# One expert's weights multiplied from split FP32R halves instead of FP32, in a fused attention and mixture-of-experts kernel

## The chip, the cores and the metric

The kernel runs on one core of a Trainium2 chip. The metric is the device time of one execution in microseconds. TensorE does the matrix products, VectorE, ScalarE and GpSimd do elementwise work, and SyncE (SP) issues most DMAs. Each engine works through its own instruction queue in order; between engines there are only semaphores.

## The reference

The input x has 4 x 1024 tokens of 256 features. It is normalised (layer norm), then three terms are added:

```python
xn = _layernorm(x, axis=-1)
x = x + _L0_attn_ref(xn, Wq, Wk, Wv) + _L0_ffn_ref(xn, w_gate, w_in, w_out)
```

The attention has 16 heads of 16 features, softmax over the keys, and a normalisation over each batch entry. The feed-forward part has 8 experts without a nonlinearity between their two layers, and each token takes the two experts with the highest logits:

```python
for e in range(E):
    h = xt @ w_in[e].T                       # hidden 1024
    y = y + gates[:, e:e + 1] * (h @ w_out[e].T)
```

Because nothing stands between the two products, the kernel multiplies the two weight matrices of an expert first (256 x 1024 by 1024 x 256) and applies the 256 x 256 composite to the tokens.

## The kernel before

**Tiling.** The tokens are 32 tiles of 128, in 8 chunks of 4 tiles. An expert's hidden dimension of 1024 is cut into two halves of 512; half i = 2e + s is one w_in tile and one w_out tile of 128 partitions x 1024 elements in FP32 (512 KB each). They land in one of 6 slots, made of the tiles wp and of the parts of xn and acc that belong to chunks 4 to 7, which are not needed yet.

**The stage of the experts.** expert_product(e, s) (L952) multiplies one half: for each of the two 128-row blocks of the composite (dh) it runs HU = 4 FP32 matmuls of 256 columns (L960), accumulating over both halves in one bank of PSUM. half_done counts finished first halves, m_ready counts finished blocks of the composite. ScalarE (m_out, L486) copies a block out rounded to FP32R, and VectorE (m_lo, L671) subtracts to get the low part, so that later products can be done as three FP32R matmuls: high x high, high x low, low x high.

**What lies between the products.** The first two chunks of tokens are handled in the same stage: token_statistics and normalise_tokens on VectorE with scale_of_chunk on GpSimd (L394) between, transposes on TensorE (L921), xt_out on ScalarE and xt_lo on VectorE, which split the transposed tokens into xth and xtl, and project_v (L948) and project_qk (L932), which are FP32R in three terms, with copies by v_out and qk_copy on ScalarE and qk_lo_half on VectorE. TensorE's order in this stage is written out by hand (L968 to L993): products 0 and 1, transposes of chunk 0, product 2, project_v of chunk 0, two blocks of project_qk, product 3, two more blocks, product 4, transposes of chunk 1, product 5, project_v of chunk 1, product 6, two blocks, product 7, two blocks, then products 8 to 15 with nothing between. ScalarE, VectorE and GpSimd have orders of their own that fit this (L538 to L559, L773 to L804, L400).

**Loads.** SP's load_weights (L278) issues the two DMAs of half i and, from i = 6 on, first waits until the product of half i - 6 is done.

**After the stage.** TensorE waits for ml_done of all experts and goes on with y_bank (L1007), the tokens times the composites, mixed with the projections of chunks 2 to 7; then attention (L1039, L1061, L1081) over 32 blocks. The tiles qf and kf hold the attention's features; GpSimd sets kf to 1.0 at the start (L392), and SP's first feature loads come after all experts.

**Tiles.** qf (128 x 4 x 1024, FP32R), kf (128 x 4 x 512, FP32R) and the third set of xth and xtl (chunk 2) are not in use while the experts' weights are multiplied.

Of the kernel before, what the change touches and what calls it, by code (L numbers as in the profile page):

```python
# [15 lines left out]
def attention_and_experts(nc, x, wq_t, wk_t, wv_t, wg_t, w_in, w_out_t, out):  # L16
# [29 lines left out]
    HELD = 4  # L46
    SETS = 3
# [10 lines left out]
    with ctx:  # L58
# [57 lines left out]
        WS = len(win)  # L116
        vb = sb("vb", [P, 2, NKT, VW])
# [55 lines left out]
        half_done = sem("half_done")  # L173
        m_ready = sem("m_ready")
# [98 lines left out]
        def _(sp):  # L273
# [108 lines left out]
        def _(pool):  # L382
# [9 lines left out]
            nc.gpsimd.memset(kf[:].bitcast(FP32), 1.0).then_inc(att_const, 1)  # L392

# [6 lines left out]
            for c in range(NC // 2):  # L400
                scale_of_chunk(c)
# [74 lines left out]
        def _(act):  # L476
# [4 lines left out]

            def m_out(e):
# [6 lines left out]
            def xt_out(c):  # L489

                if c >= SETS:
                    act.wait_ge(y_ready[-1], TC * (c - SETS + 1))
                for kt in range(KT):
# [43 lines left out]

            xt_out(0)  # L538
            m_out(0)
            for t in range(TC):  # L540
                v_out(0, t)
            for o in range(2):
                qk_copy(0, o)
            m_out(1)
            for o in range(2, 4):
                qk_copy(0, o)
            xt_out(1)
            m_out(2)
            for t in range(TC):
                v_out(1, t)  # L550
            for o in range(2):
                qk_copy(1, o)
            m_out(3)
            for o in range(2, 4):
                qk_copy(1, o)
            m_out(4)
            second_weight(0)
            for e in range(5, E):
                m_out(e)  # L559

# [65 lines left out]
        def _(dve):  # L626
# [31 lines left out]
            def xt_lo(c):  # L658
# [118 lines left out]
            nc.vector.tensor_tensor(wqkl[:], wqk, wqkh[:].bitcast(FP32), ALU.subtract).then_inc(w_lo, 1)  # L777
            xt_lo(0)
            m_lo(0)
            token_statistics(1)  # L780
            normalise_tokens(1)
            for o in range(2):
                qk_lo_half(0, o)
            m_lo(1)
            for o in range(2, 4):
                qk_lo_half(0, o)
            xt_lo(1)
            m_lo(2)
            token_statistics(2)
            normalise_tokens(2)  # L790
            for o in range(2):
                qk_lo_half(1, o)
            m_lo(3)
            for o in range(2, 4):
                qk_lo_half(1, o)
            dve.wait_ge(const_step, 6 + E)
            first_choice(0)
            second_choice(0)
            m_lo(4)
            gate_weights(0)  # L800
            token_statistics(3)
            normalise_tokens(3)
            for e in range(5, E):
                m_lo(e)  # L804
# [109 lines left out]
        def _(pe):  # L914
# [37 lines left out]
            def expert_product(e, s):  # L952

                slot = (2 * e + s) % WS
                pe.wait_ge(w_in_s[slot], 32 * ((2 * e + s) // WS + 1))
                for dh in range(KT):
                    if s == 0 and e >= 2:
                        pe.wait_ge(ml_done, KT * (e - 2) + dh + 1)
                    for h in range(HU):
                        last = nc.tensor.matmul(ps[:, M_BANK[e % 2][dh], 0:D], win[slot][:, h, dh * P:(dh + 1) * P],  # L960
                                                wout[slot][:, h, :], start=s == 0 and h == 0,
                                                stop=s == 1 and h == HU - 1)
# [226 lines left out]
```

## Time and profile before

| | us |
|---|---|
| median of 3 runs (1003.32 to 1004.2) | 1004.07 |
| profiled execution | 1001.28 |
| its span, first to last instruction | 999.5 |
| TensorE busy in the span | 974.0 |
| VectorE, ScalarE, GpSimd busy | 780.2, 694.2, 285.1 |

The profiled execution is a single one and 2.8 us below the median of the runs. All durations in the rows further down are from it. A row of a timeline has the start, the length, the engine, the line of the kernel, the operation and, in brackets, how long the engine had been idle and what released it. PE is TensorE, PEld its load of weights, DVE VectorE, ACT ScalarE, POOL GpSimd, SPq and ACTq the issue of DMAs. An FP32 matmul appears as two records.

### The profile page before, as it was taken

To read this page: it belongs to the slowest core of one execution; us is meant where nothing else is said; L and a number is where in the kernel's file an instruction comes from. 1 tells how busy PE (TensorE), PEld (TensorE's weight loads), DVE (VectorE), ACT (ScalarE), POOL (GpSimd) and SP (SyncE) were. 2 spreads that over 40 slices of the span, in tenths; PEclk is the share of its full clock that TensorE was granted. 3 is DMA by queue.
4 is the path that set the end of the run, shared out by engine and by line. 5 is a ranking of instruction groups with operands and counts; after the bars stand their busy time and mean duration, and the time that the engine had idled before them with its cause. 6 is when DMAs were issued, how large, how long until landed. Compare 5 with 4: busy or idle time off the path is not lost.

```text
span 999.5 us, 20786 instructions
## 1 busy us (share of the span) xinstructions
PE 974.0 (97%) x7816; PEld 504.5 (50%) x7816; DVE 780.2 (78%) x961; ACT 694.2 (69%) x1385; POOL 285.1 (29%) x389
## 2 busy tenths in 40 slices
PE   7999999999998999999999999999999999999994
PEld 6888888888876433333333333333333333333332
DVE  4344454543466899999999999999999999999975
ACT  2312333333322789999989899898989999899994
POOL 2001445544455222223222322223222322223222
PEclk9999999999999999999999999999999999999997
DMA  9967442223200133333333333333333333332204
GB/s 355 366 248 217 144 139 76 72 78 107 88 23 1 43 98 92 97 92 95 92 93 95 88 100 87 97 92 93 94 91 99 86 98 92 95 93 73 73 23 162
DMA packets 127043, 108.59 MB, mean 109 GB/s; under 512 B 81120, under 2 KB 102368, under 8 KB 126944
## 3 DMA queue, kind: packets, MB, share of 16 engines
q1 hardware_dynamic: 122720, 102.81, 35.4%
q10 hardware_dynamic: 4224, 4.46, 1.3%
q8 instruction: 62, 1.02, 0.4%
q14 instruction: 37, 0.30, 0.1%
HBM read 80.75 MB, written 42.21 MB: 123 GB/s over the span
## 4 chain that ended last, share of the span: by engine, by line
PE 96%; POOL 1%; DMA 1%; DVE 1%; issue 1%; ACT 0%; DVEq 0%; SPq 0%; ACTq 0%; POOLq 0%
PE ps L1081 28%; PE ps L1061 22%; PE ps L1007 18%; PE ps L1039 11%; PE ps L960 6%; PE ps L932 4%; PE ps L948 2%; PE ps L1097 1%; PE ps L1109 1%; PE ps L921 1%; DMA wp<-w_out_t 0%; DMA qf<-ot 0%; POOL rden L425 0%; ACT stage L534 0%; DVE xn L885 0%
## 5 line engine op out<-in xcount | busy, mean ns | idle before, releaser
L750 DVE TENSOR_REDUCE negm<-ps 128x1 f32<-128x1024 f32 x512 | 614.8, 1222 | 31.7 <-PE ps L1039 27.3
L585 ACT ACTIVATE wp<-ps 128x512 f32<-128x512 f32 x680 | 368.9, 595 | 43.7 <-PE ps L1061 6.7
L1061 PE MATMUL ps<-qf,kf 50*128 50x512 f32 x1024 | 373.1, 446 | 0.1
L1039 PE MATMUL ps<-kf,qf 48*128 48x512 f32 x1024 | 366.1, 444 | 1.0 <-DVE negm L750 1.0
L1061 PEld LDWEIGHTS ps<-qf,kf 50*128 50x128 f32 x1024 | 152.6, 185 | 199.0 <-ACT wp L585 97.5
L1081 PE MATMUL ps<-wp,vb 128*17 128x256 f32 x2720 | 212.6, 385 | 0.1
L1039 PEld LDWEIGHTS ps<-kf,qf 48*128 48x128 f32 x1024 | 147.2, 185 | 4.3 <-issue 3.9
L425 POOL TENSOR_TENSOR rden<-choice,minus 128x16 f32<-128x16 f32 x31 | 90.3, 2914 | 151.5 <-ACT choice L604 151.5
L585 ACT ACTIVATE picks<-ps 128x512 f32<-128x512 f32 x172 | 102.7, 597 | 22.8 <-PE ps L1061 5.0
L741 DVE SCALAR_TENSOR_TENSOR acc<-ps,gates,acc 128x256 f32<-128x256 f32 x64 | 30.8, 482 | 101.3 <-PE ps L1007 97.2
L1081 PEld LDWEIGHTS ps<-wp,vb 128*17 128x17 f32 x2720 | 46.0, 95 | 122.7 <-ACT vstage L585 53.2
L440 POOL TENSOR_TENSOR mpart<-negm,zero 128x8 fp32r<-128x8 f32 x64 | 12.9, 201 | 321.3 <-DVE negm L750 321.3
L1007 PE MATMUL ps<-mth,xth 128*128 128x512 f32 x256 | 102.6, 401 | 1.2 <-DVE stage L739 0.5
L585 ACT ACTIVATE vstage<-ps 128x512 f32<-128x512 f32 x172 | 101.8, 592 | 1.1 <-PE ps L1061 1.1
L1007 PE MATMUL ps<-mth,xtl 128*128 128x512 f32 x256 | 101.0, 395 | 0.0
L1007 PE MATMUL ps<-mtl,xth 128*128 128x512 f32 x256 | 100.9, 394 | 0.0
L534 ACT ACTIVATE wp<-ps,gates 128x256 f32<-128x256 f32 x96 | 40.3, 471 | 51.1 <-PE ps L1007 51.1
L521 ACT CAST stage<-ps 128x512 fp32r<-128x512 f32 x32 | 18.8, 587 | 60.2 <-PE ps L932 51.2
L1007 PEld LDWEIGHTS ps<-mth,xth 128*128 128x128 f32 x256 | 48.1, 188 | 14.4 <-issue 4.8
L1081 PE MATMUL ps<-picks,vb 128*17 128x256 f32 x688 | 53.9, 385 | 0.9 <-issue 0.8
L408 POOL TENSOR_TENSOR wp<-wp 128x512 f32<-128x512 f32 x24 | 31.1, 1294 | 82.8 <-ACT wp L534 82.8
L1007 PEld LDWEIGHTS ps<-mth,xtl 128*128 128x128 f32 x256 | 48.1, 188 | 11.5
(124 smaller groups left out, 898.9 us busy)
## 6 DMA issues: line engine op xcount, KB each, us to landing
qk_d<-stage SPq DMA_DIRECT2D x64, 256.0 KB
feat_d<-qk_d SPq DMA_DIRECT2D x64, 256.0 KB, 3.3
qf<-feat_d SPq DMA_DIRECT2D x128, 128.0 KB
qf<-feat_d SPq DMA_DIRECT2D x128, 64.0 KB
kf<-feat_d SPq DMA_DIRECT2D x128, 64.0 KB
v_d<-vstage ACTq DMA_DIRECT2D x8, 544.0 KB, 4.8
vb<-v_d SPq DMA_DIRECT2D x128, 34.0 KB, 2.4
acc<-x SPq DMA_DIRECT2D x8, 512.0 KB, 7.2
```

The source lines that it names most:

```text
L408: nc.gpsimd.tensor_tensor(scaled[:, 0:2], scaled[:, 0:2], scaled[:, 2:4], ALU.add).then_inc(ff_step, 1)
L425: nc.gpsimd.tensor_tensor(rden[:], rows[:, :, :, DH], minus[:], ALU.pow).then_inc(rows_step, 1)
L534: nc.scalar.activation(sums_of(t)[0][:, 2 * (j - BY_VECTOR) + h, :], ps[:, y_bank_of(t, j), h * D:(h + 1) * D], ACT.Copy, scale=gates[:, t ...
L585: nc.scalar.activation(weight_tile(n, j, b)[:, h * HALF:(h + 1) * HALF], ps[:, score_bank(score_turn[unit, b]), :], ACT.Exp).then_inc(exp_ ...
L741: nc.vector.scalar_tensor_tensor(out=total, in0=product, scalar=gate, in1=total, op0=ALU.mult, op1=ALU.add).then_inc(ff_added[j], 1)
L750: nc.vector.tensor_reduce(negm[:, n % 2, qt:qt + 1], ps[:, b:b + 2, :].rearrange("p b c -> p (b c)"), AX.X, ALU.max, negate=True).then_inc ...
L932: last = nc.tensor.matmul(ps[:, PROJECT_BANK[o % 2], :], w[:, o // 2, kt, (o % 2) * P:(o % 2 + 1) * P], v[:, c % SETS, kt, :], start=i == ...
L960: last = nc.tensor.matmul(ps[:, M_BANK[e % 2][dh], 0:D], win[slot][:, h, dh * P:(dh + 1) * P], wout[slot][:, h, :], start=s == 0 and h == ...
L1007: last = nc.tensor.matmul(ps[:, y_bank_of(t, j), :], v[:, t // TC % SETS, kt, tokens], m[:, kt, 2 * j:2 * j + 2, :].rearrange("p e d -> p ...
L1039: last = nc.tensor.matmul(ps[:, MAX_BANK[turn % 2] + half, :], qf[rows, u, qt * P:(qt + 1) * P], kf[rows, u, :], start=True, stop=True)
L1061: nc.tensor.matmul(ps[:, score_bank(score_turn[unit, half]), :], kf[rows, u, j * P:(j + 1) * P], qf[rows, u, h * HALF:(h + 1) * HALF], sta ...
L1081: last = nc.tensor.matmul(ps[32 * c:32 * c + VW, PV_BANK, 0:POS // 4], vb[:, n % 2, j + b * NKT // 2, :], weight_tile(n, j, b)[:, c * (POS ...
```

## The change

Only half 0 of the first expert stays in FP32 (WHOLE = 1). The other fifteen halves are split into a high part, rounded to FP32R, and a low part, and multiplied in three FP32R terms (24 matmuls of 256 columns in place of 8 FP32 ones). There are two sets of split tiles, used in turn: the four slots of qf, and kf with the third set of xth and xtl. ScalarE makes the high parts, GpSimd the low part of w_in, VectorE the low part of w_out. The loads wait for the split of half i - 6 instead of its product. The orders of ScalarE, VectorE and GpSimd are written anew, and GpSimd's memset of kf moves behind the last product. The order of TensorE stays.

```diff
+        flat_kf = kf[:].rearrange("p s k -> p (s k)")
+        split = [[qf[:, i, :] for i in range(4)],
+                 [flat_kf[:, 0:POS], flat_kf[:, POS:2 * POS], xth[:, SETS - 1].rearrange("p k t -> p (k t)"),
+                  xtl[:, SETS - 1].rearrange("p k t -> p (k t)")]]
...
-                if earlier >= 0:
-                    sp.wait_ge(*((m_ready, KT * (earlier // 2 + 1)) if earlier % 2 else (half_done, earlier // 2 + 1)))
+                if 0 <= earlier < WHOLE:
+                    sp.wait_ge(*((m_ready, KT) if earlier else (half_done, 1)))
+                elif earlier > 0:
+                    sp.wait_ge(w_in_low, earlier - WHOLE + 1)
+                    sp.wait_ge(w_out_low, earlier - WHOLE + 1)
...
-            nc.gpsimd.memset(kf[:].bitcast(FP32), 1.0).then_inc(att_const, 1)
...
-            for c in range(NC // 2):
-                scale_of_chunk(c)
+            def low_of_w_in(i):
+                pool.wait_ge(w_high, 2 * (i - WHOLE) + 1)
+                high, low = split[i % 2][0:2]
+                nc.gpsimd.tensor_tensor(low, win[i % WS], high.bitcast(FP32), ALU.subtract).then_inc(w_in_low, 1)
+
+            scaled_after = {0: 0, 2: 1, 6: 2, 9: 3}
+            for i in range(2 * E):
+                if i >= WHOLE:
+                    low_of_w_in(i)
+                if i in scaled_after:
+                    scale_of_chunk(scaled_after[i])
+            pool.wait_ge(m_ready, KT * E)
+            nc.gpsimd.memset(kf[:].bitcast(FP32), 1.0).then_inc(att_const, 1)
...
+            def high_of_weights(i):
+                slot = i % WS
+                act.wait_ge(w_in_s[slot], 32 * (i // WS + 1))
+                if i >= WHOLE + 2:
+                    act.wait_ge(*((m_ready, KT * ((i - 2) // 2 + 1)) if i % 2 else (half_done, (i - 2) // 2 + 1)))
+                nc.scalar.copy(split[i % 2][0], win[slot]).then_inc(w_high, 1)
+                nc.scalar.copy(split[i % 2][2], wout[slot]).then_inc(w_high, 1)
...
+            def low_of_w_out(i):
+                dve.wait_ge(w_high, 2 * (i - WHOLE) + 2)
+                high, low = split[i % 2][2:4]
+                nc.vector.tensor_tensor(low, wout[i % WS], high.bitcast(FP32), ALU.subtract).then_inc(w_out_low, 1)
...
             def expert_product(e, s):
+                i = 2 * e + s
+                if i < WHOLE:
+                    pe.wait_ge(w_in_s[i], 32)
+                    products = [(win[i], wout[i], h) for h in range(HU)]
+                else:
+                    pe.wait_ge(w_in_low, i - WHOLE + 1)
+                    pe.wait_ge(w_out_low, i - WHOLE + 1)
+                    in_high, in_low, out_high, out_low = split[i % 2]
+                    products = [(a, b, h) for h in range(HU) for a, b in ((in_high, out_high), (in_high, out_low), (in_low, out_high))]
```

ScalarE's order becomes, with high(i) for high_of_weights(i): high(1), xt_out(0), high(2), m_out(0), v_out(0, 0..3), high(3), qk_copy(0, 0..1), high(4), m_out(1), qk_copy(0, 2..3), high(5), xt_out(1), high(6), m_out(2), v_out(1, 0..3), high(7), qk_copy(1, 0..1), high(8), m_out(3), qk_copy(1, 2..3), high(9), high(10), m_out(4), then for e = 5, 6, 7: high(2e + 1), high(2e + 2) if there is one, m_out(e), with second_weight(0) after m_out(6).

VectorE's order becomes, with low(i) for low_of_w_out(i): low(1), xt_lo(0), low(2), m_lo(0), statistics and normalisation of chunk 1, low(3), qk_lo_half(0, 0..1), low(4), m_lo(1), qk_lo_half(0, 2..3), low(5), xt_lo(1), low(6), m_lo(2), statistics and normalisation of chunk 2, low(7), qk_lo_half(1, 0..1), low(8), m_lo(3), qk_lo_half(1, 2..3), low(9), token_statistics(3), low(10), m_lo(4), normalise_tokens(3), low(11), first_choice(0), low(12), m_lo(5), second_choice(0), low(13), low(14), m_lo(6), low(15), gate_weights(0), m_lo(7).

## Rows read from the trace of the kernel before

**Rows 1.** The page: busy time of each engine; the last chain by engine.

```profile
PE 974.0 (97%) x7816; PEld 504.5 (50%) x7816; DVE 780.2 (78%) x961; ACT 694.2 (69%) x1385; POOL 285.1 (29%) x389
...
PE 96%; POOL 1%; DMA 1%; DVE 1%; issue 1%; ACT 0%; DVEq 0%; SPq 0%; ACTq 0%; POOLq 0%
```

**Rows 2.** The chain that ended last, in order of time: start, length, what.

```profile
16.10 0.87 PE ps L921 x8
...
20.43 3.07 PE ps L948 x24
...
46.91 2.79 PE ps L932 x12
49.69 3.45 PE ps L960 x16
...
84.48 1.09 PE ps L921 x8
...
95.43 0.73 PE ps L948 x6
```

**Rows 3.** Table by stretches: busy us of PE, PEld, DVE, ACT, POOL; clock; DMA.

```profile
25.00:50.00 25.00, 25.00 (x129) 21.82 (x128) 9.35 (x25) 7.54 (x20) 1.21 (x2) 1.00 0.96 366
50.00:75.00 25.00, 25.00 (x117) 21.80 (x116) 12.08 (x42) 3.87 (x11) 1.21 (x2) 1.00 0.69 248
```

**Rows 4.** Groups of ScalarE by shape, 0 to 220 us: busy us, mean ns.

```profile
L495 ACT CAST xth<-ps 128x512 fp32r<-128x512 f32 x14 | 7.5, 594 | 9.8 <-PE ps L921 9.8
...
L486 ACT CAST mth<-ps 128x256 fp32r<-128x256 f32 x16 | 5.9, 376 | 31.8 <-PE ps L960 31.8
...
L480 ACT CAST wqkh<-stage 128x1024 fp32r<-128x1024 f32 x1 | 1.0, 1040 | 0.0
```

**Rows 5.** The timeline of VectorE: start, length, what, idle time before.

```profile
13.20 1.22 DVE L777 TENSOR_TENSOR wqkl<-stage,wqkh 128x1024 fp32r<-128x1024 f32 x1
...
65.03 1.41 DVE L633 BATCH_NORM_STATS2 st<-acc 128x6 f32<-128x256 f32 x4
...
67.09 0.16 DVE L645 SCALAR_TENSOR_TENSOR var<-part 128x4 f32<-128x4 f32 x1
```

**Rows 6.** GpSimd's additions by line: ns min/median/max.

```profile
L408 POOL TENSOR_TENSOR wp<-wp x24: 1287/1296/1299, 93.3 to 276.0; 128x512 f32<-128x512 f32 x24
...
L416 POOL TENSOR_TENSOR acc<-acc,wp x24: 729/738/847, 96.4 to 279.1; 128x256 f32<-128x256 f32 x24
```

**Rows 7.** The timeline at the kernel's end, VectorE and GpSimd, 993 to 997 us.

```profile
993.71 0.69 DVE L911 TENSOR_TENSOR stage<-xn,acc 128x512 f32<-128x512 f32 x1
...
994.08 1.44 POOL L472 TENSOR_TENSOR stage<-xn,acc 128x512 f32<-128x512 f32 x1 [1.19 <-ACT xn L622]
...
994.67 1.40 DVE L911 TENSOR_TENSOR stage<-xn,acc 128x512 f32<-128x512 f32 x1 [0.28 <-ACT xn L622]
```

**Rows 8.** The timeline of TensorE's weight loads in products 0 and 1.

```profile
6.08 6.05 PEld L960 LDWEIGHTS ps<-wp 128*128 128x128 f32 x16 [6.08 <-DMA wp<-w_out_t]
12.38 3.32 PEld L960 LDWEIGHTS ps<-wp 128*128 128x128 f32 x16 [0.24 <-DMA wp<-w_out_t]
```

**Rows 9.** The timeline of GpSimd after the stage of the experts.

```profile
92.07 0.20 POOL L396 TENSOR_TENSOR veps<-var,epst 128x4 f32<-128x4 f32 x1 [23.46 <-DVE var L645]
92.35 1.01 POOL L398 TENSOR_TENSOR rstd<-veps,mhalf 128x4 f32<-128x4 f32 x1
```

**Rows 10.** Table by stretches: product 0 (L960's PE and PEld), then the kernel's end.

```profile
7.00:8.00 1.00, 1.00 (x4) 0.73 (x4) 1.00 1.00 310
...
985.00:986.00 1.00, 0.39 (x4) 0.15 (x2) 1.00 (x2) 0.00 (x0) 0.00 (x0) 1.00 0.00 0
986.00:987.00 1.00, 0.00 (x0) 0.00 (x0) 0.97 (x2) 0.00 (x0) 0.00 (x0) 1.00 0.39 140
...
988.00:989.00 1.00, 0.00 (x0) 0.00 (x0) 0.28 (x1) 0.00 (x0) 0.64 (x1) 0.50 0.44 155
```

**Rows 11.** The timeline of SP's DMA issues: the first load of features.

```profile
94.58 1.51 SPq L325 DMA_DIRECT2D qf<-feat_d  x2
```

More of the change, by code:

```diff
@@ L46, in attention_and_experts @@
     HELD = 4
+    WHOLE = 1
     SETS = 3
@@ L116, in attention_and_experts @@
         WS = len(win)
+        flat_kf = kf[:].rearrange("p s k -> p (s k)")
+        split = [[qf[:, i, :] for i in range(4)],
+                 [flat_kf[:, 0:POS], flat_kf[:, POS:2 * POS], xth[:, SETS - 1].rearrange("p k t -> p (k t)"),
+                  xtl[:, SETS - 1].rearrange("p k t -> p (k t)")]]
+        split = [[part.rearrange("p (h d) -> p h d", h=HU) for part in parts] for parts in split]
         vb = sb("vb", [P, 2, NKT, VW])
@@ L173, in attention_and_experts @@
         half_done = sem("half_done")
+        w_high = sem("w_high")
+        w_in_low = sem("w_in_low")
+        w_out_low = sem("w_out_low")
         m_ready = sem("m_ready")
@@ L546, in _ @@
                 qk_copy(0, o)
+            high_of_weights(5)
             xt_out(1)
+            high_of_weights(6)
             m_out(2)
@@ L555, in _ @@
                 qk_copy(1, o)
+            high_of_weights(9)
+            high_of_weights(10)
             m_out(4)
-            second_weight(0)
             for e in range(5, E):
+                high_of_weights(2 * e + 1)
+                if e + 1 < E:
+                    high_of_weights(2 * e + 2)
                 m_out(e)
+                if e == E - 2:
+                    second_weight(0)
             for t in range(NT - 1):
@@ L777, in _ @@
             nc.vector.tensor_tensor(wqkl[:], wqk, wqkh[:].bitcast(FP32), ALU.subtract).then_inc(w_lo, 1)
+            low_of_w_out(1)
             xt_lo(0)
+            low_of_w_out(2)
             m_lo(0)
@@ L781, in _ @@
             normalise_tokens(1)
+            low_of_w_out(3)
             for o in range(2):
                 qk_lo_half(0, o)
+            low_of_w_out(4)
             m_lo(1)
@@ L786, in _ @@
                 qk_lo_half(0, o)
+            low_of_w_out(5)
             xt_lo(1)
+            low_of_w_out(6)
             m_lo(2)
@@ L790, in _ @@
             normalise_tokens(2)
+            low_of_w_out(7)
             for o in range(2):
                 qk_lo_half(1, o)
+            low_of_w_out(8)
             m_lo(3)
@@ L795, in _ @@
                 qk_lo_half(1, o)
+            low_of_w_out(9)
             dve.wait_ge(const_step, 6 + E)
+            token_statistics(3)
+            low_of_w_out(10)
+            m_lo(4)
+            normalise_tokens(3)
+            low_of_w_out(11)
             first_choice(0)
+            low_of_w_out(12)
+            m_lo(5)
             second_choice(0)
-            m_lo(4)
+            low_of_w_out(13)
+            low_of_w_out(14)
+            m_lo(6)
+            low_of_w_out(15)
             gate_weights(0)
[L801 to L804, printed above, removed]
+            m_lo(7)
             for t in range(NT - 1):
@@ L958, in expert_product @@
                         pe.wait_ge(ml_done, KT * (e - 2) + dh + 1)
[L959 to L962, printed above, removed]
+                    for k, (a, b, h) in enumerate(products):
+                        last = nc.tensor.matmul(ps[:, M_BANK[e % 2][dh], 0:D], a[:, h, dh * P:(dh + 1) * P], b[:, h, :],
+                                                start=s == 0 and k == 0, stop=s == 1 and k == len(products) - 1)
                     if s == 1:
```

10 lines of the change are left out of this document (8 added, 2 removed).

## The prediction

> **What bounds the kernel now.** I began with the page's busy line: TensorE is busy 974 of 999.5 us, VectorE 780, ScalarE 694, GpSimd 285 [rows 1]. TensorE's work also makes up 96% of the chain that ended last [rows 1], so anything taken from the matmuls, or put between them, moves the end one for one. The chain in order of time shows the stage that the change touches. It runs from the first product to the transposes of the third chunk at 84.48 [rows 2], and TensorE stands idle only for the first weights and for about 1 us at its end. The table by stretches shows the engines that get new work: in 25 to 75 us VectorE is busy 21.4 of 50, ScalarE 11.4, GpSimd 2.4 [rows 3]. There is room in total, so what decides is latency: how soon a half of an expert is ready, not how full the engines are. I number the halves 0 to 15 (i = 2e + s).
>
> **What is removed.** Fifteen of the sixteen halves run in FP32 now, 8 matmuls of 256 columns each, and one half takes 3.45 to 3.46 us [rows 2]. After the change a half is 24 matmuls on FP32R values. The nearest row is the projection of V, FP32R with 264 columns: 6 in 0.73 us, 0.122 each [rows 2]. Eight columns fewer are 3 ns less, 0.119, so a half takes 24 x 0.119 = 2.86 us. The projection's first block, 24 in 3.07 us [rows 2], is the upper end. The gain is 15 x 0.60 = 9.0 us; with the upper end it is 5.8.
>
> **What is added, per half.** ScalarE rounds both tiles (128x1024): the same cast takes 1.04 us [rows 4]. VectorE's subtraction of this shape takes 1.22 us [rows 5]. GpSimd's subtraction has no row of this shape. Its additions take 1.296 us for 512 elements and 0.738 for 256 [rows 6], a slope of 2.18 ns an element, so 1.296 + 512 x 2.18 ns = 2.41 us. The ends are 1.3 (the row of 512 elements, if length cost nothing) and 2.6 (twice that row); I take the slope.
>
> Do the two subtractions run side by side? Near the end of the trace VectorE's L911, with two SBUF inputs, meets GpSimd's L472, also with two. L911 takes 0.69 us at other times and 1.40 here; it started at 994.67 and ended at 996.07, which is 0.55 after GpSimd's 995.52 [rows 7]. So the later one stood until the earlier was through, and then did nearly its whole work. GpSimd begins its half 1 us ahead of VectorE, so VectorE ends 1.22 - 0.14 = 1.08 after it. The Trainium skill says so as a general rule (SBUF — State Buffer, Who interferes with whom): two SBUF inputs on VectorE contend with a GpSimd instruction that reads SBUF, and whichever issues second blocks fully. Only these rows bear on it here; by the rule it would happen in all fifteen halves, and without it the sum would be that of the third rival.
>
> From the start of ScalarE's first cast a half is ready after 1.04 + 2.41 + 1.08 = 4.53, with hand-overs 4.6 us. That is more than a product (2.86), and there are only two sets of split tiles: the casts of half i wait for the end of product i-2.
>
> **Where TensorE now waits.** I go through the queues in their new order.
> - Product 1: its load of weights waits for the DMA until 12.38 today [rows 8], so they have landed at 12.4. ScalarE casts to 13.4. VectorE's L777, also with two SBUF inputs, runs until 14.4 [rows 5] and holds GpSimd back; GpSimd ends at 16.7, VectorE at 17.8. Product 0 ended at 12.1 [rows 8]: 5.7 us idle, of which 0.3 exists today.
> - Product 2: product 1 ends at 20.7, the transposes (0.87 [rows 2]) at 21.5. The casts of half 2 are queued on ScalarE behind the two copies of those transposes (0.59 each [rows 4]), so they begin at 22.2 and the product at 26.9: 5.4 idle.
> - Product 3: queued behind v_out(0, 3), a small copy and one of 0.38 [rows 4], and the DMA issue after it: I put 1.1 us after the last projection of V. TensorE has only two blocks of Q (2.79 [rows 2]) to fill 1.1 + 4.6: 2.9 idle.
> - Product 5: queued behind qk_copy(0, 3). TensorE has product 4 and the transposes, 3.7 us, against 0.7 + 4.6: 1.6 idle. Products 4, 6, 7 and 8 have enough other work ahead of them: none.
> - Product 9: behind qk_copy(1, 3), with only product 8 as cover: 0.8 + 4.6 - 2.9 = 2.5 idle.
> - Product 10: GpSimd's scale_of_chunk(3) now stands before its subtraction and waits for VectorE's statistics of chunk 3, which stand behind low_of_w_out(9). Those take 2.2 (65.03 to 67.25 [rows 5]), the two small GpSimd operations 1.3 [rows 9], then 2.41: 5.9 after half 9 was ready, against 2.9 of product 9: 3.0 idle.
> - Products 11 to 15: now bare products. Start to start of every second one is its own 2.86 plus the split: 0.2 + 4.6 for even halves, and 0.75 more for odd ones, whose casts are queued behind m_out (two copies of 0.37 [rows 4]). That is 7.7 or 8.4 us for two, 6.9 today. Followed through, with VectorE's expert choice between, they start about 81.1, 85.5, 89.1, 93.1 and 97.3: 5.2 idle in all.
>
> Sum of the new idle time: 5.4 + 5.4 + 2.9 + 1.6 + 2.5 + 3.0 + 5.2 = 26.0. Less 9.0: **17 us later** at the transposes.
>
> **TensorE's clock.** The first product's weight loads took 6.05 us where the next product's took 3.3 [rows 8]: the engine came from idleness and ran it mostly at the lower level, 1.2 GHz (the granted clock reads 1.00 there [rows 10], so it is the durations that tell). At the end of the kernel TensorE does its last 0.39 us of work in 985 to 986; the granted clock is still 1.00 in 986 to 987 and 0.50 in 988 to 989 [rows 10]. The two idle times of 5.4 and 5.7 us around product 1 are twice as long as this, so I expect the clock to be at 1.2 GHz when products 1 and 2 begin. By 6.05 against 3.46 (1.75) each costs 2.1 more, and the transposes between 0.7: 5 us together. Bounds: 0, and about 11 if the idle times of 2.5 to 3 us before products 3, 9 and 10 do it as well. I take 5. The Trainium skill says that how many matmuls run cold varies between runs of one kernel (TensorE: Matmul & The Clock Gate, Part 1); by it the sum would be anything from 17 to 22, and one trace can't show that.
>
> **What costs nothing.** SP's loads now wait for the split of i-6 in place of product i-6. Load 10 still lands some 10 us before its cast at 69, since the casts come late. GpSimd's memset of kf (1.8 us) moves behind the last product; features(0) waits for it, but in the trace that began 10 us after the products, behind the regroup transfers [rows 11], which hide it. GpSimd's next work comes 7.6 us after the transposes' start, at 92.07 [rows 9]. gate_weights hides behind product 15. From the transposes on the code is the same and TensorE has no gap there to take up a delay, so all of it reaches the end.
>
> The profiled execution took 1001.28 us (span 999.5). It becomes 1001.3 + 17 + 5 = 1023.3. The median of the runs shown is 2.8 above it: 1026 us.
>
> **Rivals.** (1) The clock stays up: 1004.1 + 17 = 1021. For it: no row shows a pause of this length in the middle of work. (2) It falls in the 3 us pauses too: 1004.1 + 17 + 11 = 1032. For it: 988 is less than 3 us after the last matmul [rows 10]. (3) The subtractions run side by side: a split takes 3.5 (GpSimd's alone), product 1 is not held by L777, and the idle time falls from 26 to 17: 1004.1 + 8 = 1012, up to 1015 with the clock. Against it: [rows 7]. (4) Faster: the splits keep ahead of TensorE, so that only product 1's waits, bare at 1.04 + 2.41 = 3.5 us: 1004.1 - 9.0 + 3.5 = 998.6. It decides from the point where a split takes less than a product; cast and GpSimd's subtraction alone are 3.45 against 2.86, and in today's order the casts stand behind copies that wait for TensorE. (5) The change does not do what it says: FP32R at 3.07 or slower a half, by the load of weights. Then it is 3 us more than the forecast, 1029; it is in the range.
>
> **How the numbers follow.** Forecast 0.42, rival 1 0.22, rival 2 0.17, rival 3 0.11, rival 4 0.02, rival 5 0.03; 0.03 for something between that cancels out. The range of 8 in 10 reaches from rival 3's upper part to just above rival 2: 1013 to 1034. A measurement tells about 0.2% (2 us) from no change. Only rival 4 is faster, 0.02; same 0.02; slower 0.96.
>
> **What would show it.** In the profile after: L960's matmuls three times as many, about 0.12 us apart; TensorE idle before them some 26 us, released by VectorE's subtraction of wout (or GpSimd's for product 10), above all before products 1 and 2; VectorE's new subtraction at a median near 2.5 us though the work is 1.22, if the two exclude each other, and 1.22 if rival 3 holds; a granted clock below 1.00 at 15 to 28 us; the transposes L921 of chunk 2 near 101 to 107 instead of 84.5, and all later stages shifted by the same amount. The prediction is wrong if GpSimd's 128x1024 takes far from 2.4 us, or if a later stage gives time back.

## The result

The kernel became slower: 1033.3 us in the median (1032.2 to 1034.5) against 1003.7, a ratio of 1.0295 with a 95% interval of 1.0277 to 1.0313. The prediction was 1026 us with a range of 1013 to 1034. The time lies less than 1 us inside the upper end of the range, and direction and mechanism held; the forecast was 7 us too low, and the second rival (1032), in which the clock falls in the shorter pauses too, came nearest.

The page of the changed kernel, in the same order as [rows 1]: span, busy time, the last chain by engine.

```profile
span 1031.9 us, 21121 instructions
...
PE 977.7 (95%) x7936; PEld 512.6 (50%) x7936; DVE 820.0 (79%) x976; ACT 722.9 (70%) x1415; POOL 323.7 (31%) x404
...
PE 89%; DVE 4%; ACT 2%; POOL 2%; issue 1%; DMA 1%; SPq 0%; DVEq 0%; ACTq 0%; POOLq 0%
```

TensorE's share of the chain is 89% (96% before) and VectorE, which had 1%, has 4%. To see where, the table by stretches is cut at the transposes of the third chunk, where the stage of the experts ends: at 116.73 us here, at 84.48 before [rows 2]. Columns: length; busy us (instructions) of PE, PEld, DVE, ACT and POOL; granted clock; share of the DMA engines; GB/s. First the changed kernel, then the kernel before.

```profile
0.00:116.70 116.70, 81.25 (x488) 75.44 (x488) 75.19 (x121) 47.77 (x78) 45.41 (x42) 0.87 0.68 241
```
```profile
0.00:84.50 84.50, 77.49 (x369) 67.14 (x369) 35.27 (x106) 19.10 (x48) 7.72 (x27) 1.00 0.85 314
```

The stage is 32.2 us longer. TensorE is idle 35.4 us in it instead of 7.0, and it is busy 3.8 us more, though its matmuls should take 9 us less. What follows the transposes takes 915.2 us against 915.0: nothing is lost or given back there. The profiled execution grew by 32.4 us (span 999.5 to 1031.9); the medians differ by 29.6, since the profiled execution of before was 2.4 us faster than that kernel's median. It is also faster than each of the 41 other executions of that kernel on record (1002.5 to 1006.9 us), so against a usual execution every kernel below stands 1 to 6 us better than against this trace; in which stage these lie no trace shows.

TensorE's timeline shows each pause, in brackets (L1036 is now the line of all products, L718 VectorE's low part of w_out, L414 GpSimd's low part of w_in, L990 the transposes). Half 1 comes first, then 2, 3, 5, 7, 9, 10, 12, 13 and 15, then the transposes. A row that says x24 is a whole half.

```profile
17.76 0.55 PE L1036 MATMUL ps<-xth,kf 128*128 128x256 f32 x1 [6.62 <-DVE xtl L718]
...
29.39 4.87 PE L1036 MATMUL ps<-qf 128*128 128x256 f32 x24 [5.27 <-DVE qf L718]
...
43.06 0.36 PE L1036 MATMUL ps<-xth,kf 128*128 128x256 f32 x1 [2.86 <-DVE xtl L718]
...
55.73 0.36 PE L1036 MATMUL ps<-xth,kf 128*128 128x256 f32 x1 [1.52 <-DVE xtl L718]
...
68.45 0.36 PE L1036 MATMUL ps<-xth,kf 128*128 128x256 f32 x1 [0.86 <-DVE xtl L718]
...
79.61 0.36 PE L1036 MATMUL ps<-xth,kf 128*128 128x256 f32 x1 [2.40 <-DVE xtl L718]
...
86.25 5.41 PE L1036 MATMUL ps<-qf 128*128 128x256 f32 x24 [3.53 <-POOL qf L414]
...
96.44 3.11 PE L1036 MATMUL ps<-qf 128*128 128x256 f32 x24 [1.92 <-issue]
...
101.46 0.38 PE L1036 MATMUL ps<-xth,kf 128*128 128x256 f32 x1 [1.91 <-DVE xtl L718]
...
111.20 0.36 PE L1036 MATMUL ps<-xth,kf 128*128 128x256 f32 x1 [2.27 <-DVE xtl L718]
...
116.73 1.09 PE L990 MATMUL ps<-ident,xn 128*128 128x128 f32 x8 [0.92 <-DVE mtl L724]
```

The pauses before products 1 to 3 are 6.6, 5.3 and 2.9 us. The first includes 0.7 because product 0 began earlier than in the trace of before; product 1 starts at 17.76, and 17.8 was forecast. The rows of products 2 and 10 (x24) last 4.87 and 5.41 us, that of product 12 3.11: the same 24 matmuls at two clocks. The granted clock in the stretches of products 1, 4, 10, 11 and 13 says which:

```profile
17.70:23.30 5.60, 5.54 (x26) 5.58 (x27) 0.00 (x0) 0.00 (x0) 0.00 (x0) 0.51 1.05 396
...
50.30:53.30 3.00, 3.00 (x27) 2.99 (x26) 1.09 (x3) 2.48 (x3) 1.19 (x1) 1.00 0.52 186
86.20:91.50 5.30, 5.25 (x25) 5.26 (x26) 5.16 (x9) 0.00 (x0) 2.37 (x1) 0.51 0.00 0
91.50:94.40 2.90, 2.90 (x26) 2.82 (x24) 0.80 (x3) 2.26 (x3) 1.53 (x1) 1.00 0.00 0
...
101.40:105.50 4.10, 4.04 (x21) 4.07 (x22) 3.38 (x2) 0.61 (x2) 2.14 (x1) 0.58 0.66 237
```

Products 1, 10 and 13 ran mostly at 0.50, which is 1.2 GHz; products 4 and 11, which followed work without a pause, at 1.00, which is 2.4 GHz.

GpSimd's subtractions of halves 1 and 2, then three stretches of VectorE: the low parts of halves 1 and 2, and the four instructions of normalise_tokens(3).

```profile
13.35 3.18 POOL L414 TENSOR_TENSOR kf<-wp,kf 128x1024 fp32r<-128x1024 f32 x1 [2.31 <-ACT kf L510]
...
25.82 2.34 POOL L414 TENSOR_TENSOR qf<-xn,qf 128x1024 fp32r<-128x1024 f32 x1 [9.29 <-ACT qf L510]
...
81.67 1.12 POOL L406 TENSOR_TENSOR veps<-var,epst 128x4 f32<-128x4 f32 x1 [3.30 <-DVE var L692]
```
```profile
14.25 3.36 DVE L718 TENSOR_TENSOR xtl<-wp,xth 128x1024 fp32r<-128x1024 f32 x1
...
26.72 2.52 DVE L718 TENSOR_TENSOR qf<-xn,qf 128x1024 fp32r<-128x1024 f32 x1 [1.09 <-ACT qf L511]
...
83.91 5.45 DVE L701 TENSOR_SCALAR xn<-acc,mean,rstd 128x256 f32<-128x256 f32 x4 [0.33 <-POOL rstd L408]
```

GpSimd needs 2.34 us where nothing is in its way (2.41 was worked out from [rows 6]), and 3.18 where VectorE's L830 (L777 before, [rows 5]) was under way. VectorE's subtraction, 1.22 us of work, takes 2.52: it begins at 26.72 and ends at 29.24, 1.08 after GpSimd's 28.16. That is the exclusion of [rows 7], met again in eleven of the fifteen halves (VectorE's instruction took over 2 us there). And four instructions of normalise_tokens take 5.45 us, where they took 1.38 before: these have a single input in SBUF, and the prediction had not counted them. The trace of before has a sign of it. At 96.26 us, where GpSimd's additions run (one of them from 96.42, for 0.85 us), the four take 1.80 us:

```profile
96.26 1.80 DVE L654 TENSOR_SCALAR xn<-acc,mean,rstd 128x256 f32<-128x256 f32 x4
```

### The profile page after: what moved, and what is told of

The parts are those of the page before. It is cut to its first block, busy times and chain, and to the rows that moved or that the text cites. A ratio compares the mean times of both kernels' runs of the same rounds, so it can differ in the third digit from the quotient of the medians.

```text
span 1031.9 us, 21121 instructions
## 1 busy us (share of the span) xinstructions
PE 977.7 (95%) x7936; PEld 512.6 (50%) x7936; DVE 820.0 (79%) x976; ACT 722.9 (70%) x1415; POOL 323.7 (31%) x404
## 4 chain that ended last, share of the span: by engine, by line
PE 89%; DVE 4%; ACT 2%; POOL 2%; issue 1%; DMA 1%; SPq 0%; DVEq 0%; ACTq 0%; POOLq 0%
PE ps L1156 27%; PE ps L1136 22%; PE ps L1082 17%; PE ps L1114 11%; PE ps L1001 4%; PE ps L1036 3%; PE ps L1017 2%; PE ps L1172 1%; PE ps L1184 1%; DVE xtl L718 1%; DVE qf L718 1%; PE ps L990 1%; DMA acc<-x 1%; DVE st L680 0%; DMA qf<-ot 0%
## 5 line engine op out<-in xcount | busy, mean ns | idle before, releaser
L1156 PE MATMUL ps<-vstage,vb 128*17 128x256 f32 x688 | 53.9, 385 | 0.0
```

The source lines that it names most:

```text
L1156: last = nc.tensor.matmul(ps[32 * c:32 * c + VW, PV_BANK, 0:POS // 4], vb[:, n % 2, j + b * NKT // 2, :], weight_tile(n, j, b)[:, c * (POS ...
```

## The experiments

Each experiment is compared with runs of the kernel before on the same chip (medians of 1003.8 to 1004.3 us; 1003.7 for the change itself). The ratio is worked out from all runs and can differ from the quotient of the medians by up to 0.2%. "Transposes" is the start of the transposes of the third chunk in the profiled execution, 84.5 before and 116.7 after the change. In the experiments a list SPLIT of the halves to split stands in place of WHOLE. With it half 1 is split into the slots of qf and half 2 into kf, the other way round than in the changed kernel; no run shows what this alone does.

| kernel | transposes at | median us | ratio to before (95%) |
|---|---|---|---|
| the change | 116.7 | 1033.3 | 1.0295 (1.0277 to 1.0313) |
| 1 pauses filled | 108.0 | 1026.8 | 1.022 (1.0203 to 1.0237) |
| 2 both low parts on VectorE | 100.3 | 1020.7 | 1.0161 (1.0143 to 1.0178) |
| 3 halves 0 to 2 in FP32 | 102.6 | 1020.6 | 1.016 (1.0145 to 1.0175) |
| 4 splits made, not used | 95.9 | 1030.2 | 1.0259 (1.0243 to 1.0275) |
| 5 FP32R products, no pauses | 79.2 | 999.8 | 0.9955 (0.9939 to 0.997) |
| 6 casts of half 2 first | 109.7 | 1027.4 | 1.023 (1.0212 to 1.0247) |
| 7 as 4, loads not held | 96.1 | 1016.5 | 1.0126 (1.0105 to 1.0146) |
| 8 eleven halves, new orders | 81.2 | 1001.0 | 0.9957 (0.9941 to 0.9974) |
| 9 as 8, VectorE's order | 80.3 | 1000.4 | 0.9971 (0.9958 to 0.9983) |
| 10 normalisation first | 118.9 | 1037.7 | 1.0332 (1.0309 to 1.0355) |

### 1. The pauses filled with dummy matmuls

```diff
+                for _ in range(FILL.get(i, 0)):
+                    nc.tensor.matmul(ps[:, bank, 0:D], wvgh[:, 0, 0:P], wvgh[:, 0, 0:D], start=True, stop=True)
                 if i < WHOLE:
```

> The changed kernel, with dummy matmuls (256 columns, FP32R, result unused, into a free bank) on TensorE ahead of the waits of products 1, 2, 3, 5, 9, 10, 12, 13, 14 and 15: 40, 40, 20, 10, 18, 24, 10, 5, 8 and 8 of them, at 0.12 us each less than the pause that each wait had. They give TensorE work in the pauses and nothing else. Theory (the clock falls in the pauses and the products after them run slow): TensorE's busy time in the stage rose by 3.8 us although cheaper matmuls should have taken 9 off, so the clock costs some 12.6 us; with the clock kept up the time is 1033 - 12 = 1021 us, and products 1, 2, 3, 10, 13 and 15 take 2.9 us instead of 4.6 to 5.4. Rival (the products are slow for another reason, such as reading weights from tiles just written, or the pauses alone make up the loss): 1033 us, the products as slow as before. If the dummies outlast the pauses, the time is in between.

It took 1026.8 us, 6.5 less than the changed kernel; 12 were expected, and 0 by the rival. The table by stretches to the transposes (the 672 matmuls of TensorE include 183 dummies), then products 1 and 11:

```profile
0.00:108.00 108.00, 92.28 (x672) 86.69 (x672) 77.03 (x121) 47.94 (x78) 45.87 (x42) 1.00 0.71 254
```
```profile
18.16 3.11 PE L1048 MATMUL ps<-qf 128*128 128x256 f32 x24 [1.71 <-DVE qf L724]
...
85.88 3.11 PE L1048 MATMUL ps<-qf 128*128 128x256 f32 x24 [1.40 <-DVE qf L724]
```

The granted clock is 1.00 throughout and each product takes 2.9 to 3.1 us. So the slow products are the clock's doing, and the rival is out. But the stage became only 8.8 us shorter (product 1 began 0.4 us later in this execution, so it is 9.2 from there). While a product runs slowly, the split of the next half goes on; take the slowness away, and TensorE waits longer instead. Without the dummies (183 of 0.12 us) TensorE is busy 70.3 us here against 81.3 in the changed kernel, and what it waits or fills is 37.7 us against 35.4. The slow clock and the pauses are therefore not a sum: the clock added some 11 us to TensorE's work (not the 12.6 of the expectation, which took off 9 us for the cheaper matmuls where busy time fell by 7.2), and 8.8 is what it cost.

### 2. Both low parts on VectorE

```diff
-                    low_of_w_in(i)
...
+                dve.wait_ge(w_high, 2 * SPLIT.index(i) + 1)
+                nc.vector.tensor_tensor(low, win[i % WS], high.bitcast(FP32), ALU.subtract).then_inc(w_in_low, 1)
+                high, low = split[SPLIT.index(i) % 2][2:4]
                 dve.wait_ge(w_high, 2 * SPLIT.index(i) + 2)
                 nc.vector.tensor_tensor(low, wout[i % WS], high.bitcast(FP32), ALU.subtract).then_inc(w_out_low, 1)
```

> The changed kernel, with both low parts made on VectorE, GpSimd doing none of the split. Theory (VectorE and GpSimd exclude each other, so a split takes 1.04 + 2.41 + 1.08 = 4.5 us from the first cast): now a split takes 1.04 + 1.22 + 1.2 = 3.5 us, each of some ten pauses shrinks by 1 us, product 10 no longer waits behind the small GpSimd operations (2 us), and some of the slow products become fast: 1033 - 12 to - 18, 1015 to 1021 us. Rival (the two ran side by side and VectorE's longer instruction is only a longer record): GpSimd's 2.4 us was the longer arm, a split then took 3.5 us already, and nothing changes: 1031 to 1035 us.

It took 1020.7 us, at the upper end of what the theory gave (1015 to 1021). One engine doing both is 12.6 us faster than two engines doing one each. TensorE's waits for the splits, in total us, times and longest, then the stage:

```profile
PE ps L1042 <- DVE qf L724: 14.1, 7, 6.5
...
PE ps L1042 <- DVE xtl L724: 4.2, 1, 4.2
```
```profile
0.00:100.30 100.30, 74.20 (x488) 68.04 (x488) 69.03 (x136) 47.73 (x78) 8.60 (x27) 0.95 0.74 267
```

Each of VectorE's subtractions takes 1.22 us here. Two engines that shut each other out gave no more than one, and GpSimd's 2.4 us stood in the place of VectorE's 1.2. Of the 16.4 us by which the transposes come earlier, 9.4 are less idle time of TensorE and 7.0 less busy time, since only products 1 and 2 ran slowly. The edit also frees the normalisation and the small GpSimd operations ahead of product 10; what each of these is worth by itself was not tested.

### 3. Halves 0, 1 and 2 in FP32

```diff
-    WHOLE = 1
+    SPLIT = [3, 4, 5, 6, 7, 8, 9, 10, 11, 12, 13, 14, 15]
```

> The changed kernel with halves 0, 1 and 2 in FP32 (split from half 3 on), all orders as they are. Theory: the two longest pauses (5.4 us each beyond today's) go with the slow clock behind them (products 1 and 2 and the transposes between, 5 us); products 1 and 2 cost 0.6 more each: 1033 - 10.8 - 5 + 1.2 = 1018 to 1020 us. Rival (later pauses absorb the time that is won ahead of them, since the rest of the stage is bound by the loads of weights or the splits): 1028 to 1033 us.

It took 1020.6 us, just above the 1018 to 1020 of the theory. The first two halves that the change split cost 12.7 us of the 29.6, against 14.6 by the steps for products 1 and 2; the transposes come 14.2 us earlier. Later pauses did not take it back.

### 4 and 7. The splits made, and not waited for

```diff
-                if i < WHOLE:
+                if True:
                     pe.wait_ge(w_in_s[i % WS], 32 * (i // WS + 1))
                     products = [(win[i % WS], wout[i % WS], h) for h in range(HU)]
...
+            sp.wait_ge(w_in_low, len(SPLIT))
+            sp.wait_ge(w_out_low, len(SPLIT))
             for c in range(NC // 2, NC):
                 load_x(c)
```

The two waits on SP are needed here, because a product that doesn't wait no longer says that its tiles have been read for the split. In the seventh experiment they are `SPLIT.index(2 * WS - 1) + 1` in place of `len(SPLIT)`.

> All fifteen splits are made in the new orders of ScalarE, GpSimd and VectorE, but TensorE multiplies the FP32 tiles as before the change and waits for no split. Theory (what costs is TensorE's wait for each split and the clock after it, not the work on the other engines): 1004 to 1009 us, a few us for the copies of transposes and projections that now stand behind casts. Rival (the added work itself holds up the chain, by its load on ScalarE and VectorE): 1015 to 1025 us.

> The fourth experiment again, with the loads of x and the stores behind them no longer held by the last splits (they wait only for the splits of the first twelve halves). All splits are made, TensorE multiplies the FP32 tiles and waits for none of them. In the fourth experiment the transposes of the third chunk came 11 us late and another 17 us went in later stages, where SP's queue of loads and stores had been put behind the last split. Theory: the 17 us were SP's queue, and the rest is the queues of ScalarE and VectorE (two pauses, 3.9 and 6.0 us): 1004 + 11 = 1012 to 1018 us. Rival (the load on the engines as such): 1025 to 1031 us.

The fourth took 1030.2 us, far from the 1004 to 1009 of the theory and above the rival's 1015 to 1025 as well. The trace said that two things were mixed. The stage was 11.4 us longer, and 17.3 us more went after it. TensorE's longest wait after the transposes:

```profile
PE ps L1015 <- DVE stage L746: 10.1, 1, 10.1
```

The 10.1 us are a wait for a block of the later projections. Its tile waits for the stores of the chunk before, which stand in SP's queue behind the loads of features, and all of those behind the loads of x, which I had put behind the last split. With only that moved (experiment 7) the time is 1016.5 us, within 1012 to 1018. So a wait that I added on a queue that "only loads" cost 14 us, at a place where nothing had been changed: TensorE's wait ends at 163.0 us, 67 after the transposes.

The 11.7 us that stay in the stage are a correction to the prediction. TensorE waits for no split here, and still stands:

```profile
33.88 0.73 PE L1015 MATMUL ps<-xth,wqkh 128*128 128x512 f32 x2 [3.90 <-DVE stage L746]
...
83.03 7.14 PE L1050 MATMUL ps<-xn 128*128 128x256 f32 x32 [0.48 <-DVE mtl L737]
...
96.14 1.97 PE L1004 MATMUL ps<-ident,xn 128*128 128x128 f32 x8 [5.96 <-DVE mtl L737]
```
```profile
26.51 5.46 DVE L712 TENSOR_SCALAR xn<-acc,mean,rstd 128x256 f32<-128x256 f32 x4 [1.41 <-POOL rstd L410]
```
```profile
33.90:38.50 4.60, 4.60 (x13) 3.67 (x14) 3.02 (x5) 0.59 (x1) 0.00 (x0) 0.63 0.91 337
```

3.9 us before a block of Q and 6.0 before the transposes (0.9 of these before the change too), both for VectorE, whose copies stand in its queue behind other work. Before the block of Q that work is normalise_tokens(1), 5.46 us instead of 1.38 while GpSimd subtracts from 26.4 to 31.2, and a subtraction; before the transposes it is the last subtraction (2.52 us instead of 1.22) and gate_weights. And the clock fell twice: the two blocks behind the first pause take 4.60 us instead of 2.96, the granted clock reads 0.63 there, and the transposes take 1.97 instead of 1.09. So the added work does hold up the chain by itself, through the order of VectorE's queue and the exclusion; how much each of the two has was not separated. VectorE is busy 77 of these 96 us, where it was busy 35 of 84.5 before.

### 5. The cheaper matmuls without pauses

```diff
+                if i > 4:
+                    pe.wait_ge(w_in_s[i % WS], 32 * (i // WS + 1))
+                    in_high, in_low, out_high, out_low = split[(i - 3) % 2]
```

> What the cheaper matmuls are worth with no pause at all. Halves 0, 1 and 2 stay in FP32; only halves 3 and 4 are split (both low parts on VectorE, casts early enough to be ready), and halves 5 to 15 are multiplied with those two split pairs again, so that they need no split of their own (the composites of the experts from 5 on are left out in that sense: they are made from the wrong weights). The loads and everything else stay. Theory (each half as 24 FP32R matmuls takes 2.86 us instead of 3.45): 13 x 0.59 = 7.7 us less than before the change, 996 to 997 us. Rival (a half is held back by the load of weights or by PSUM to 3.07 us or more): 999 to 1001 us.

Halves 5 to 15 are multiplied with the wrong weights, so it is the composites of experts 2 to 7 that this kernel leaves out. TensorE's rows of half 1, of the block of Q that waits, and of the transposes:

```profile
13.19 3.72 PE L1040 MATMUL ps<-wp 128*128 128x256 f32 x16 [2.52 <-DMA wp<-w_out_t]
...
31.20 0.73 PE L1001 MATMUL ps<-xth,wqkh 128*128 128x512 f32 x2 [1.15 <-DVE stage L737]
...
79.21 1.09 PE L990 MATMUL ps<-ident,xn 128*128 128x128 f32 x8 [0.92 <-DVE mtl L728]
```

The transposes come at 79.2, 5.3 us earlier than before the change. Two things went against it: the weights of half 1 landed 0.8 us later in this execution (13.19 against 12.38, [rows 8]), and one block of Q waited 1.15 for VectorE. Without them it is 7.2, close to the 7.7 expected; the rival's slower rate is not there. The median of 999.8 us is 4 us below before, not 7. What follows the transposes takes 918.6 us here, 3.6 more than before, at the full clock up to the last stage. TensorE's waits in it:

```profile
PE ps L1195 <- DVE bmv L919: 5.0, 1, 5.0
...
PE ps L1001 <- DVE stage L737: 1.8, 1, 1.8
PE ps L1140 <- DMA qf<-ot: 1.0, 3, 0.4
```

The first row was 4.7 before, the other two did not exist: together 3.1 of the 3.6 us. But the profiled executions differ by 1.7 us (1001.28 against 999.57) where the medians differ by 4.1, so some 2.4 of the 3.6 us can come from the unusually fast profiled execution of before. L1001 is the later projections, which wait for a copy of VectorE, and L1140 waits for the reloads of the attention's results. That these belong to the edit itself, and not to this execution alone, was not tested.

### 6. The casts of half 2 ahead of the copies of the transposes

```diff
-            xt_out(0)
             high_of_weights(2)
+            xt_out(0)
...
-            xt_lo(0)
             low_of_w_out(2)
+            xt_lo(0)
```

> The changed kernel with one place moved: the casts of half 2 stand on ScalarE ahead of the two copies of the transposes (xt_out), and its low part on VectorE ahead of xt_lo. Theory (the pause before product 2 is only a matter of the queue: the weights landed at 16.4, but the casts stand behind copies that wait for TensorE, which waits for product 1's split): the pause of 5.3 us goes, and product 2 no longer starts at the low clock: 1033 - 5.3 - 2 = 1024 to 1028 us. Rival (the pause moves to the projection of V or to product 3, since those wait for ScalarE and VectorE, which have the same work to do): 1031 to 1034 us.

It took 1027.4 us, 5.9 less. In its trace TensorE has no pause before product 2 any more, and product 3 starts at 35.9 us instead of 43.1:

```profile
35.94 0.48 PE L1041 MATMUL ps<-qf 128*128 128x256 f32 x2 [2.85 <-DVE qf L723]
```

The transposes come 7.1 earlier too, so nothing later took it back. The pause was a matter of place in a queue alone.

### 8 and 9. A version from the findings

```diff
-    WHOLE = 1
+    SPLIT = [3, 4, 5, 6, 7, 8, 9, 11, 12, 14, 15]
```

with both low parts on VectorE and the casts ahead of copies where there was a choice: on ScalarE high(3) after m_out(0), high(4) after v_out(0, 3), high(5) after m_out(1), high(9) after m_out(3), high(11) before m_out(4). VectorE's order follows it; its expert choice for chunk 0 now stands ahead of low(11), and the statistics and normalisation of chunk 3 stand behind low(12) and low(14).

> A version made from the findings: both low parts on VectorE, only the eleven halves 3 to 9, 11, 12, 14 and 15 split, the others in FP32 (so that each split has at least 6 us from when its tiles come free), and the casts ahead of copies that wait for TensorE where there is a choice. Theory (a split of 3.5 us that is ready before TensorE asks costs nothing, and the clock stays up): 11 x 0.59 = 6.5 us less than before the change, 997 to 999 us. Rival (some pause of 1 to 3 us is left, from VectorE's queue, which has 27 us more to do, and the clock falls once): 1001 to 1006 us.

It took 1001.0 us, 0.43% faster than before (0.26% to 0.59%), less than the 997 to 999 expected.

```profile
31.30 0.73 PE L1001 MATMUL ps<-xth,wqkh 128*128 128x512 f32 x2 [1.20 <-DVE stage L737]
...
50.25 3.11 PE L1036 MATMUL ps<-qf 128*128 128x256 f32 x24 [0.52 <-DVE qf L722]
...
81.23 1.09 PE L990 MATMUL ps<-ident,xn 128*128 128x128 f32 x8 [0.92 <-DVE mtl L728]
```

The transposes come at 81.2, 3.3 us earlier than before. Of the 6.5 us the weights of half 1, 0.9 late, two waits for VectorE (1.2 and 0.5) and some tenths between took the rest. Experiment 9 moved the two instructions that caused these waits:

```diff
-            low_of_w_out(4)
             for o in range(2):
                 qk_lo_half(0, o)
+            low_of_w_out(4)
...
-            normalise_tokens(2)
             low_of_w_out(7)
+            normalise_tokens(2)
```

> The eighth experiment with two places of VectorE's order moved: qk_lo_half(0, 0..1) ahead of the low parts of half 4, and the low parts of half 7 ahead of normalise_tokens(2). In the eighth, TensorE stood 1.2 us before the third block of Q and 0.5 us before product 7, and its transposes of the third chunk came 3.2 us before those of the kernel before the change. Theory (both pauses were VectorE's queue): 1.7 us less, 999 to 1000 us. Rival (the pauses move to the next wait): 1001 us again.

```profile
51.78 0.72 PE L1001 MATMUL ps<-xth,wqkh 128*128 128x512 f32 x2 [2.20 <-DVE stage L737]
...
80.31 1.09 PE L990 MATMUL ps<-ident,xn 128*128 128x128 f32 x8 [0.92 <-DVE mtl L728]
```

Both waits are gone, and a new one of 2.2 us stands 20 us on, again for VectorE. Its 1000.4 us cannot be told from those of experiment 8 (intervals 0.9958 to 0.9983 and 0.9941 to 0.9974): the rival was right. Either version is faster than the kernel before, by 0.2% to 0.6% with the intervals of both, and than the changed one by some 32 us.

### 10. The normalisation ahead of GpSimd's subtraction

```diff
                 pool.wait_ge(w_high, 2 * SPLIT.index(i) + 1)
+                if i in (7, 10):
+                    pool.wait_ge(xn_done, 12 if i == 7 else 16)
```

> The changed kernel, with GpSimd's subtractions of halves 7 and 10 made to wait until VectorE's normalisation of chunk 2 and 3 is through. In the changed kernel one of these VectorE instructions took 2.5 us instead of 0.41 while GpSimd subtracted. Theory (the normalisation too, though it has one input, is shut out by GpSimd): each of its instructions in this stage goes back to 0.40 to 0.43 us; the time hardly moves, since GpSimd's work is then later by as much: 1031 to 1036 us. Rival (the long ones have another cause, such as the DMA writing next to them): some instruction stays above 1 us.

VectorE's four instructions of normalise_tokens, chunks 2 and 3:

```profile
63.04 1.38 DVE L706 TENSOR_SCALAR xn<-acc,mean,rstd 128x256 f32<-128x256 f32 x4 [1.40 <-POOL rstd L408]
...
84.54 1.37 DVE L706 TENSOR_SCALAR xn<-acc,mean,rstd 128x256 f32<-128x256 f32 x4
```

Back to 1.38 and 1.37 us, from 3.48 and 5.45. So they were shut out by GpSimd's subtraction, and the DMA is no cause. The time is 1037.7 us in the median of two runs, a little worse than the 1031 to 1036 that I allowed. Product 10 waits 4.7 us instead of 3.5, since GpSimd starts later; and product 9 runs slowly here (4.60 us instead of 3.11, granted clock 0.64) behind a pause of 2.4 us that left the clock up in the changed kernel. This order does not win it back.

## Why the prediction was right, and where it was not

**What bounds the kernel.** Right: TensorE carries the chain, the stage's end moved by 32.2 us and the kernel's by 32.4. But 22 were forecast, and the sign given for the transposes (101 to 107 us) failed: they came at 116.7. The 10 us that are missing are 6.5 of waiting and 3.8 of clock, as worked out below.

**The number.** The profiled execution was forecast at 1023.3 us and took 1033.7, 10.4 more. In the median the error is 7.3 only because 2.8 us were added for the distance between profiled execution and median, which is 2.4 in the kernel before and -0.4 in the changed one. That the time lies within the range owes something to this luck.

**What is removed.** Right: 2.86 us a half were forecast, and undisturbed halves follow each other at 0.12 us a matmul; experiment 5 found 7.2 of 7.7 us.

**What is added.** Right to a few hundredths: cast 1.05, GpSimd 2.34 to 2.39, and VectorE through 1.08 after GpSimd, as forecast from [rows 7]. The Trainium skill (SBUF — State Buffer, Who interferes with whom) was borne out in its general form for the subtractions. Its list also names tensor_scalar as an instruction that, under conditions on its operands, can take the shared ports though it has one input; the normalisation's 2.5 us for one instruction, instead of 0.41, and experiment 10 agree. The prediction used the rule for the subtractions only.

**Where TensorE waits.** The pauses were forecast as 5.7, 5.4, 2.9, 1.6, 2.5 and 3.0 us before products 1, 2, 3, 5, 9 and 10; they are 6.6, 5.3, 2.9, 1.5, 2.4 and 3.5. Two steps failed in size. Product 7 was to have none and has 0.9: normalise_tokens(2) stood in VectorE's queue ahead of the low part and was itself held by GpSimd. And with no clock effect at all (experiment 1) the transposes come at 108.0 where the sum gives 101.5: 6.5 us more. By the start of product 10 it is 3.5 (81.3 against 77.8, which is the sum's 97.3 for product 15 less 5.2 of idle time and five products of 2.86), by product 11 4.8 and by product 13 6.6. In the trace of experiment 1 each step has an instruction held by GpSimd or VectorE ahead of it: normalise_tokens(2) before product 7 (3.58 us instead of 1.38), GpSimd's small addition before product 10 (1.11 instead of 0.20), normalise_tokens(3) before product 11 (5.50), and before product 13 one instruction of the expert choice with two inputs in SBUF (0.23 us at other times; GpSimd subtracts from 90.42 to 92.83):

```profile
90.79 2.12 DVE L768 SCALAR_TENSOR_TENSOR picks<-picks,choice 128x64 f32<-128x64 f32 x1
```

So the prediction applied the exclusion to the subtractions and left out the other instructions that meet one of them. What each is worth by itself was not tested; experiment 10 frees the two normalisations and gains nothing.

**The clock.** The kind was right and the size too small. Products 1 and 2 took 5.3 and 4.7 us to the start of what follows them, 2.4 and 1.9 more than 2.86, where 2.1 each was forecast; the transposes between them were hardly slowed (granted clock 0.93). But the low clock did not need the two long idle times alone: it came back for products 3, 10, 13 and 15, after pauses of 1.9 to 3.5 us. That is rival 2 in kind, though that had named products 3, 9 and 10. I had taken 5 us with a bound of 11; experiment 1 gives 8.8 at the transposes and 6.5 in the median. The bound held, the value taken was too low: [rows 10] had shown a fall within 3 us after the last work, and I applied it to the two longest pauses alone. It is not certain either: after the pauses before products 5, 9 and 12 (1.5, 2.4 and 1.9 us) the clock stayed up. In experiment 3, product 9 ran slowly behind the same pause of 2.4 us:

```profile
66.20:70.90 4.70, 4.60 (x24) 4.43 (x24) 3.44 (x12) 0.37 (x1) 2.48 (x3) 0.64 0.65 223
```

**What costs nothing.** Mostly right: nothing is lost after the stage, and no product waited for weights. But "room in total" was too kind: experiment 7 shows 11.7 us from VectorE's queue, the exclusion and the clock with no wait for a split.

**The rivals.** The first is out (the clock fell), the second came nearest: the clock fell behind short pauses too, if not behind all that it named. The third is out (experiment 2). The fourth, faster, is out for this order, though experiments 5 and 8 are faster than the kernel before: where TensorE does not have to wait for the splits, most of the gain is there. The fifth is out (experiment 5).

## What to carry to other kernels

Before splitting FP32 work into cheaper terms, compare the time from "tiles are free" to "split is ready" with one unit of the consumer's work; if it is longer and there are only two buffers, the consumer waits wherever it has no other work, here before five of the last seven products, though no other engine was busy for more than 65% of the stage. Two elementwise subtractions on VectorE and GpSimd with operands in SBUF were done one after the other here (2.52 us instead of 1.22), and giving both to the faster engine won 12.6 us; look at every VectorE instruction that a long GpSimd one can meet, not only at the new pair. And TensorE can pay twice for a pause: once for itself, once for the slower clock behind it (some 11 us of slow work in this stage, of which 8.8 reached its end, because the next split went on meanwhile).

## What the runs showed of the hardware that was not expected

The clock can fall in a pause of 1.9 us that the kernel before has as well. In the attention's first step TensorE waits 1.9 us for GpSimd (maxima_to_rows). In the profiled execution of before the granted clock stays 1.00 there; in that of experiment 8 it does not. The table by stretches, experiment 8, 302 to 309 us:

```profile
302.00:303.00 1.00, 0.00 (x0) 0.00 (x0) 1.00 (x2) 0.00 (x0) 0.92 (x3) 1.00 0.00 0
303.00:304.00 1.00, 0.52 (x3) 0.48 (x4) 1.00 (x1) 0.00 (x0) 0.35 (x2) 1.00 0.00 0
...
305.00:306.00 1.00, 1.00 (x4) 0.80 (x3) 0.00 (x0) 0.36 (x1) 0.00 (x0) 0.50 0.04 8
...
308.00:309.00 1.00, 1.00 (x6) 0.82 (x5) 0.00 (x0) 0.84 (x2) 0.00 (x0) 1.00 0.00 0
```

TensorE works again from 303.5, the clock is at 0.50 in 305 to 306, and back at 1.00 in 308 to 309. The work behind the transposes took 917.9 us in this execution instead of 915.0; it was 918.9 in experiment 2, where the clock fell twice there, 916.5 in experiment 9, where it fell once, and 915.2 in the changed kernel, where it did not fall. So the same code differs by 1 to 4 us, and falls of the clock at its own short pauses go with the longer times; they are not all of it, since experiment 5 took 918.6 us with the clock up. Of the twelve traces, this one pause (1.85 to 1.87 us in each) is followed by the low clock in five (experiments 1, 2, 4, 8 and 9) and not in seven. That fits experiment 8, which gained 3.3 us in the stage and 0.4 in its profiled execution, and the single executions of experiment 9, between 998.6 and 1004.9 us: a gain of 0.3% needs many runs. What decides whether a given pause brings the clock down is left open.

A small GpSimd addition of 128x4, 0.20 us at other times [rows 9], took 1.12 us at 81.67 in the changed kernel while VectorE's subtraction (81.51, 1.22 us) ran: the exclusion works both ways, and a short instruction waits for the end of the long one (82.79 and 82.73).
